# Spreading one layer norm's three steps, and two gate steps, over later steps of a hand-written pipeline

## The reference, cut to what matters

```python
def _mab(q, k, v, p):                      # used twice: h = _mab(ind, x, x, p1); _mab(x, h, h, p2)
    x = q + _mha(_ln(q, g1, b1), _ln(k, g1, b1), _ln(v, g1, b1), ...)
    h = _ln(x, g2, b2)                     # the input of the second feed-forward, for p2
    ff = gelu(h @ l1w.T + l1b) @ l2w.T + l2b
    return x + ff
...
h = h + attn(layernorm(h))                 # then, for the experts:
gw = topk_gate(x @ wg_group, 2, 4)         # softmax over the two largest of four groups
iw = topk_gate(z @ wg_inner[g], 2, 8)      # and over the two largest of eight experts
```

## Time and profile before

| | |
|---|---|
| time, median of 3 runs | 2388.35 us (2387.33 to 2389.3) |
| profiled execution | 2404.56 us, of which the span of the trace is 2402.7 |
| PE, DVE, ACT, POOL busy over the span | 84%, 56%, 48%, 32% |
| tower | up to about 1350 us |
| `induce` | about 1350 to 1963 us |
| experts | about 1963 us to the end |

### The profile page before, as it was taken

The page is one execution under the profiler, slowest core; times in us unless marked ns, Lnnn a source line. Parts: engine busy times, 40 slices in busy tenths (PEclk is TensorE's granted clock), DMA queues, the critical chain, the costliest instruction groups (busy, mean ns, idle before and its releaser), DMA issues. The chain is left out here.

```text
span 2402.7 us, 44240 instructions
## 1 busy us (share of the span) xinstructions
PE 2019.5 (84%) x14601; PEld 1445.8 (60%) x14601; DVE 1340.1 (56%) x4495; ACT 1156.6 (48%) x2495; POOL 778.4 (32%) x975
## 2 busy tenths in 40 slices
PE   5799999999999999999998367887676329999986
PEld 4466666666566666666565245554443219999972
DVE  2365556555665656555663246777566505555547
ACT  2476666665666666656663024544433204443434
POOL 0012222122222222122222111234566725555546
PEclk7799999999999999999998667787866559999995
DMA  3641334123432344124300233452121157777754
GB/s 99 123 73 26 54 67 67 38 31 67 68 55 50 55 67 67 40 29 67 67 1 1 79 74 81 78 93 44 44 50 39 55 171 243 230 227 217 212 151 146
DMA packets 113988, 207.11 MB, mean 86 GB/s; under 512 B 23076, under 2 KB 47654, under 8 KB 113112
## 3 DMA queue, kind: packets, MB, share of 16 engines
q1 hardware_dynamic: 102616, 184.90, 34.3%
q0 software_dynamic: 10176, 17.09, 2.2%
q10 hardware_dynamic: 976, 2.30, 0.4%
HBM read 147.59 MB, written 64.66 MB: 88 GB/s over the span
## 5 line engine op out<-in xcount | busy, mean ns | idle before, releaser
L679 ACT ACTIVATE tower_prob<-tower_prob,tower_negmax 128x386 f32<-128x386 f32 (+1 forms) x768 | 390.5, 556 | 303.4 <-DVE tower_negmax L886 302.7
L886 DVE CUSTOM_DVE_ANT_0 tower_prob<-tower_sbank,tower_band 128x386 f32<-128x386 f32 (+1 forms) x768 | 346.2, 488 | 141.5 <-PE tower_sbank L453 136.2
L491 PEld LDWEIGHTS tower_tbank<-tower_ident,tower_prob 128*128 128x128 f32 x1920 | 228.2, 143 | 129.5 <-issue 81.7
L491 PE MATMUL tower_tbank<-tower_ident,tower_prob 128*128 128x128 f32 x1920 | 284.8, 279 | 22.1 <-DVE tower_probT L911 20.4
L735 ACT ACTIVATE tower_probT<-tower_tbank 128x384 f32<-128x384 f32 (+1 forms) x576 | 227.6, 430 | 127.4 <-PE tower_tbank L491 125.3
L2052 POOL DMA_INDIRECT scratch_yt<-experts_y,experts_rows x190 | 186.7, 983 | 185.1 <-DVE experts_y L2195 117.0
L430 PE MATMUL tower_dbank<-tower_oxT,tower_w 96*128 96x512 f32 x384 | 191.5, 624 | 13.9 <-ACT tower_oxT L724 13.9
L2110 PE MATMUL experts_ybank<-experts_w,experts_hid 128*128 128x128 f32 x1520 | 185.1, 275 | 0.0
L2098 PE MATMUL experts_hbank<-experts_zT,experts_w 128*128 128x256 f32 x760 | 183.7, 385 | 1.1 <-ACT experts_zT L2134 1.1
L453 PE MATMUL tower_sbank<-tower_k_st,tower_q_st 49*128 49x386 f32 (+1 forms) x768 | 161.2, 414 | 25.7 <-POOL tower_k_st L635 14.3
L2143 ACT ACTIVATE experts_hid<-experts_hbank,experts_w 128x256 f32<-128x256 f32 x190 | 79.7, 470 | 202.9 <-PE experts_hbank L2098 147.8
(11 more groups left out here) (314 smaller groups left out, 3447.2 us busy)
## 6 DMA issues: line engine op xcount, KB each, us to landing
experts_w<-ew SPq DMA_DIRECT2D x95, 578.0 KB
scratch_qk<-tower_qk SPq DMA_DIRECT2D x64, 384.0 KB, 4.6
tower_q_st<-scratch_qk SPq DMA_DIRECT2D x96, 192.0 KB, 7.8
tower_k_st<-scratch_qk SPq DMA_DIRECT2D x96, 192.0 KB, 10.7
experts_rows<-scratch_zs SPq DMA_DIRECT2D x95, 132.0 KB
scratch_kq<-induce_kq SPq DMA_DIRECT2D x8, 1024.0 KB, 4.3
experts_res<-scratch_yt SPq DMA_DIRECT2D x8, 1024.0 KB, 6.8
induce_k_st<-scratch_kq SPq DMA_DIRECT2D x48, 128.0 KB, 4.3
```

Source lines behind the costliest of these rows:

```text
L491: mm = pe.transpose(bank[:, jb * P:jb * P + P], prob[:, hg % PR, at + jb * P:at + jb * P + P], ident[:, :])
L679: act.activation(prob[:, hg % PR, 0:width(i)], prob[:, hg % PR, 0:width(i)], ACT.Exp, bias=negmax[:, hg % PR:hg % PR + 1], scale=-1.0).the ...
L886: scores.copied(dve.tensor_tensor_reduce(prob[:, hg % PR, 0:width(i)], bank[:, 0:width(i)], band[:, BAND_AT[i]:BAND_AT[i] + width(i)], sca ...
```

## The change

Six step numbers move and the exponential gets one of its own. Nothing is added to or removed from the computation. The three pieces of the norm before the second feed-forward go from 85, 86, 88 to 86, 89, 93 (its consumer UP2 stays at 98). The exponential goes from 111 to 114, so that ACT now issues it behind Z_COPY. RANK, COEF and SLOT go two steps later, STORE two, and SCATTER one.

```diff
-        Y2_MOM, Y2_NORM, Y2_SUM, Y2_T = 85, 86, 87, 88
+        Y2_MOM, Y2_NORM, Y2_SUM, Y2_T = 86, 89, 87, 93
         UP2, DOWN2, Z_NORM, X5_NORM, Z_ROWS, Z_T = (98, 99), 101, 103, 105, 104, 106
-        GATE, GATE_1, GATE_2, Z_COPY, RANK, COEF, SLOT, STORE = 108, 109, 111, 112, 113, 114, 115, 118
-        SCATTER = range(119, 135)
+        GATE, GATE_1, GATE_2, Z_COPY, GATE_EXP, RANK, COEF, SLOT, STORE = 108, 109, 111, 112, 114, 115, 116, 117, 120
+        SCATTER = range(120, 136)
...
-                if p == GATE_2:
+                if p == GATE_EXP:
                     act.wait_ge(gexp_in, m + 1)
                     act.activation(gs[:, 3, :], gs[:, 2, :], ACT.Exp).then_inc(gexp_out, 1)
```

## The result

The changed kernel took 2376.06 us (median of 13 runs, 2368.69 to 2384.03) against 2388.35 us for the kernel before (median of 13, 2384.63 to 2395.4): ratio 0.995, interval 0.9936 to 0.9964. It is faster by 12.3 us, less than half of the 28 us forecast, and 15.7 us above the predicted 2360.4.

The account below looks back on a forecast made before the run. Chains of waits, not a full engine, bound the rounds, with PE idle 41.3 us for yn. Round gains summed to 27.8, say 28 us, taking the median from 2388.35 to 2360.4; range 2345 to 2380 for 8 in 10.

Parts of the forecast that it names:

- the forecast's own 2350 to 2371: Range of the main forecast, chance 0.63, allowing collisions of 0 to 2.6 us in five rounds and SLOT's 1 us.
- the terms of rounds 1 and 2: Gains of 4.5 us in round 1, where DVE soon becomes the limit, and 3.5 in round 2 after collisions.
- The norm of y2: Late rounds on DVE: zn starts at 1784.8, not 1787.26, and x5 is ready at 1788.1, not 1793.2; gain 5.1 us.
- The two y2b additions keep their place behind POOL's roots and three scatters and now come after x5: On POOL, read from round 4: the additions no longer run beside x5, which then takes 1.1 us.
- Collisions at the gate: DVE's first gate operations meet POOL's scaling of z; bounded by 0 and 2.6 us a round, taken as 1.2.
- The new wait at Y2: Y2's product claims the rank product's bank, freed by DVE only in COEF; costs 2.7 us once, in round 0.
- The rank product between the up products: On PE, the first up product runs in the wait for `chosen`; gains 1.6 us in rounds 3 to 5.
- Round 6, 3 us: Last round: POOL's idle before its double root caps the gain at 3.8; 3 taken, as x5 was not delayed.
- One scatter more ... is covered by the 14 us before the padding ends: End of `induce` on POOL: one scatter more, 1.26 us, behind the last double root, costs nothing.
- a gain before the last count goes to the end whole: End of `induce`: time gained ahead of DVE's last counts reaches the experts' start undiminished, as counts and padding set the end.
- The time from the last count to the end should not move.: Sign expected in the changed profile: the stretch behind DVE's last counts keeps its length.
- the wait moves on: Rival: PE's idle for yn becomes idle for zn and x5, paced by POOL; gain 10 us, 2378, chance 0.16.

Follow-up runs that it names:

- first_old_third: Changed kernel with item 0 alone keeping its old norm steps, timed as reference on the chip of another experiment: 2383.81 us, ratio 0.992.
- before_side: The kernel before, unchanged, profiled once for its stretches on one chip: 2398.67 us, one run.
- after_again: The changed kernel, unchanged, run for a second profile and more timed rounds: 2391.11 us, ratio 0.9945 to the kernel before.
- before_again: The kernel before, unchanged, run for a second profile: 2405.03 us, one run.
- sum_91_not_item0: Changed kernel with item 0's norm steps old and the y2b additions at step 91 for items 1 to 7 alone: 2380.65 us, ratio 0.9916.
- norm_only: The kernel before with only the norm's three steps moved to 86, 89, 93: 2390.44 us, ratio 0.9937.
- old_gate_side: Changed kernel with item 0's norm steps old and without the gate's part, in the four-kernel comparison on one chip: 2370.01 us, ratio 0.9919.
- first_old_side: Changed kernel with item 0 alone keeping its old norm steps, in the four-kernel comparison on one chip: 2370.98 us, ratio 0.9926.
- gate_only: Changed kernel with the norm's steps left at the old 85, 86, 88: 2398.54 us, ratio 0.9974 to the kernel before.
- changed_side: The changed kernel, unchanged, in the four-kernel comparison on one chip: 2377.79 us, ratio 0.995 to the kernel before.
- scatter_only: The kernel before with only the store of the slots and the sixteen scatters one step later: 2403.07 us, ratio 0.9986.
- norm_91: The changed kernel with the norm's step at 91 in place of 89, for all items: 2383.04 us, ratio 0.99 to the kernel before.
- turn_only: The kernel before with only the turn of the normalised rows at step 93 in place of 88: 2404.88 us, ratio 0.9995.
- sum_91_side: Changed kernel with item 0's norm steps old and all y2b additions at 91, in the four-kernel comparison on one chip: 2376.68 us, ratio 0.9946.
- old_item0_sum_91: Changed kernel with item 0's norm steps old and POOL's y2b additions at step 91 in place of 87, earlier timing: 2384.66 us, ratio 0.992.

## Why the prediction was wrong

The direction and the mechanism of the late rounds held: zn ahead of yn, x5 clear of the additions. The size did not. The time lies inside the stated range, but outside the forecast's own 2350 to 2371; the range held because it had been widened to take in a rival whose mechanism is not what happened, and that is luck.

Three steps failed. The first is a term that the sum doesn't have: the work was moved in eight items, but priced only in the seven rounds that begin with item 0's h2. The eighth is item 0 itself, whose norm lies in the opening, and there it costs 7 to 8 us. The second is the terms of rounds 1 and 2: 8.0 us forecast, 2.0 measured. The third is smaller, the end of the phase: the later scatters, put at nothing because the padding would cover them, cost some 3 us where it doesn't (by one pair of profiles).

| term | forecast | first_old_third against before_side | after_again against before_again |
|---|---|---|---|
| opening | 0 | -1.2 (item 0 left out) | -7.8 |
| round 0 | 2.5 | 0.8 | 1.0 |
| round 1 | 4.5 | 0.9 | 1.0 |
| round 2 | 3.5 | 1.1 | 1.0 |
| round 3 | 5 | 7.9 | 5.5 |
| round 4 | 5.5 | 5.1 | 6.0 |
| round 5 | 3.8 | 3.1 | 2.5 |
| round 6 | 3 | 0.1 | 0.1 |
| sum | 27.8 | 17.7 | 9.3 |

The sums are of these stretches alone. The times of the same kernels differ otherwise too: `induce` itself begins anywhere from 1337.7 to 1347.0 us in the profiles, behind a tower that no edit touched.

- *The norm of y2: zn forward by 2.5 us, x5 by 5.1.* Right in rounds 3 and 4, to 0.1 us. In rounds 5 and 6 zn came 2.5 us forward, as forecast, but x5 only 2.5 too, since it had not been delayed there (1.11 us in the kernel before in both); the prediction says this of round 6 alone. The gate's copy came 3.2 us forward in round 5, and the round gained 3.1.
- *"The two y2b additions keep their place behind POOL's roots and three scatters and now come after x5".* Wrong in round 1. That place was read from round 4, where three scatters stand ahead of the additions. In round 1 none does: the additions start at 1652.14, x5 at 1653.74, and x5 takes 3.89 us. yn then takes 2.20 beside z, ahead of a maximum that TensorE needs for the score product before the gate products. x5 ends 11.3 us behind h2, where the kernel before had 14.8, and the gate's copy came 2.1 us earlier (19.4 us behind h2 for 21.5), not 4.5. sum_91_not_item0 showed it: without the additions there x5 took 3.14 us, now beside z, yn 1.29, and the gate's copy came 16.0 us behind h2.
- *In round 2* x5 took 1.25 us, as forecast, but yn 2.83 beside the additions, again ahead of a maximum. Moving the additions did not shorten this round, so what limits it stays open.
- *Collisions at the gate, 1.2 us a round.* They were there: in round 6 L1724 took 2.15 us and L1725 1.29 beside L1482 and L1485 (plain length 0.32), 2.8 us, at the upper bound; in round 5 they came to 1.4. In round 4 there was none. The rule of the Trainium skill ("SBUF — State Buffer", "Who interferes with whom"), that such pairs block each other for a whole instruction, agrees with these rows and with x5's 3.89 us. Its 2.6 us a round did not come in every round.
- *The new wait at Y2, 2.7 us once.* The wait is as forecast, 3.39 us at L1095 in round 0 alone. Its price was more than 2.7: norm_only, which doesn't have it, has 46.4 us in round 0, after_again 50.4; old_gate_side has 48.4, first_old_side 51.5. That is 3.1 to 4.0 us.
- *The rank product between the up products, 1.6 us in rounds 3 to 5.* The wait for `chosen` is gone, as forecast, but one of 3.30 us for o2 stands at the up products. Round 4 took 37.1 us with the new rank step and 38.9 in norm_only, so the term was right there. gate_only, with the old norm, has 43.2 as before_again does, so the term needs the moved norm. Given back in round 0, it is nothing net.
- *Round 6, 3 us.* Without the later additions it took 34.4 to 34.6 us on the four slower chips, with the norm moved or not, and 30.3 to 30.8 in the changed kernel's own profile and in changed_side, first_old_side and old_gate_side on the faster chip; with the additions at 91 it took 29.4 to 30.5 on any of three chips. From the start of the last down product to h2 went 3.85 us in the changed kernel's profile, 7.33 in the kernel before and 7.96 in first_old_third, though the product's records show 3.81 in all three and a granted clock of 1.00. What makes the difference stays open, and so does what the kernel before would show on the faster chip, where it has no profile.
- *"One scatter more ... is covered by the 14 us before the padding ends", and "a gain before the last count goes to the end whole".* The 14 us were read from a profile with the time of the slower chips. In the changed kernel's profile the padding ends 12.7 us before the last scatter, and the experts' first instruction on POOL starts 3.2 us behind that scatter. first_old_side and old_gate_side show the same on one chip, and what the gate's part costs there: from DVE's copy of the last counts to the start of the last scatter it is 33.6 us with the later steps and 30.4 without. No forecast term had this 3.2 us. This is one pair of profiles; the two medians differ by 1.0 us. On the slower chips the padding ended last, as read, with the later scatters inside it.
- *"The time from the last count to the end should not move."* From DVE's copy of the last counts to POOL's first instruction of the experts it took 46.3 us in the kernel before and 37.7 in the changed one. Most of that is the chip: 46.9 us in before_side and first_old_third both, 46.7 in scatter_only, and 34.5 to 38.0 on the faster chip. But on one chip it also differs for no reason that a run isolates: 45.1 in before_again, 40.2 in after_again, 47.4 in norm_only, and 40.1 in sum_91_not_item0. It makes up 9.2 of the 16.8 us between the profiles of one kernel on two chips, first_old_third and first_old_side, and so part of the 16.2 us by which the prediction's profile lay above its median without a reason given.

The lower bound of the forecast's own range does not follow from its working: no collisions in five rounds would give 6 us more, so 2354 and not 2350. Of the rivals, the time of 2376 fits "the wait moves on" (2378), but its mechanism is not what happened: rounds 4 and 5 gained 5 to 6 and about 3 us. What stays open is why the gate's part alone gave 6 us: its rounds are only 2.1 shorter than before_again's, and its opening of 243.9 is near the kernel before's shortest, 244.3.

The best versions are the changed kernel with item 0's norm left in its old place (0.9898 to 0.9926 in three timings), the same without the gate's part (0.9919, 0.9924), and norm_91 (0.99), which changes one number. They cannot be told apart; the first two beat the changed kernel by about 7 us on one chip, norm_91 was not timed beside it.

## What to carry to other kernels

In a pipeline over items, a step that moves is moved in the fill and the drain too. Price each of those by its own rows, where the engine that takes the work may have no idle time (here the opening), or where another engine's work ends last (here the scatters). When two engines' waits have one cause, ask whose order is behind it: the wait of 41 us that TensorE showed was worth nothing to TensorE (turn_only), and everything to the engine that it waited for. And read a late round's neighbours only for late rounds: the place of an instruction on a queue depends on what the other items put ahead of it.

## What the runs showed of the hardware

- A wait that grew from 0.4 to 0.7 us to 1.73 to 1.75, on an engine that was otherwise busy, stood at the start of some 17 to 24 us at 1.2 GHz, in all five profiles taken with item 0's norm at step 89 (granted clock 0.57 to 0.65 from 1560 to 1580 us). In the profiles without it that window has 0.91 or more, but for one: sum_91_side has 0.78, while the same kernel in old_item0_sum_91 has 0.91. The price of such a stretch, 7 to 8 us, is several times the wait's length.
- The Trainium skill ("TensorE: Matmul & The Clock Gate", "A second HAM failure mode: psum-queue depth-cycling") says that frequent short idles between groups of matmuls can make the clock swing between its levels. The trace agrees in part: a wait of 1.73 to 1.75 us stands at the fall, but it is one wait and one long fall and not a repeated swing. Why this wait and not others of its length does so, no run here shows.
- Whether DVE and POOL operations lengthen each other is set by where they fall: the operations of the search with two inputs, 0.32 to 0.38 us in the changed kernel's round 4, took 1.29 to 2.15 us beside POOL's additions and scalings in its round 6 and in round 5 of sum_91_not_item0.
- One kernel's executions differ by 5 to 18 us on one chip, and the chips' medians of the kernel before by up to 19 us. Pairs of ratios taken on two chips erred by 4 us; four kernels side by side on one settled what they could not.
